# Event places, step orders, the last quarters and the first stacking of keys in a fused attention and FFN kernel

## The reference

```
x = x + xattn(layernorm(x), ctx)          # q, k, v projections, softmax over 1601 keys, output projection and bias
x = x + ffn(layernorm(x))                 # gate and up 256 -> 704, silu(gate) * up, down 704 -> 256
fp4_linear(x, w) = einsum(fp4(x), fp4(w)) # blocks of 16: scale = max|x|/6, values rounded to an FP4 grid
```

## Time and profile before

| | us |
|---|---|
| runs of before | 3369.82, 3375.37, 3386.15 (median 3375.37) |
| the profiled execution | 3376.89 |
| its span | 3375.1 |

### The profile page before, as it was taken

One profiled execution on the slowest core, in us unless ns is written; L12 is line 12 of the kernel. 1 busy time (PEld: TensorE's weight loads), 2 busy tenths in 40 slices (PEclk: granted clock), 3 DMA queues, 4 the chain that ended last, 5 costly groups with the idle time before them and its releaser, 6 DMA issues.

```text
span 3375.1 us, 55778 instructions
## 1 busy us (share of the span) xinstructions
PE 3209.6 (95%) x19606; PEld 1657.6 (49%) x19606; DVE 2698.0 (80%) x6009; ACT 2282.7 (68%) x4692; POOL 1097.4 (33%) x1411
## 2 busy tenths in 40 slices
PE   6899999999999999999999999999999999999996
PEld 4344544545455454544545455454544545454444
DVE  6877788888887878878887888878878888887855
ACT  2666677676766767767676776767767677766761
POOL 0213333243333333324343333333333333332332
PEclk6998999999999999999999999999999999999987
DMA  3332133232222322133232222322133232222200
GB/s 78 71 54 47 36 60 56 35 65 39 52 48 40 66 45 50 36 59 58 35 65 35 51 53 42 64 45 53 35 58 56 35 66 43 46 48 46 41 14 8
DMA packets 120783, 163.29 MB, mean 48 GB/s; under 512 B 47125, under 2 KB 93606, under 8 KB 120506
## 3 DMA queue, kind: packets, MB, share of 16 engines
q1 hardware_dynamic: 120506, 159.73, 27.0%
HBM read 46.22 MB, written 8.39 MB: 16 GB/s over the span
## 4 chain that ended last, share of the span: by engine, by line
PE 72%; DVE 11%; ACT 4%; SPq 4%; DMA 4%; POOL 2%; issue 2%; POOLq 0%; DVEq 0%; ACTq 0%
PE out_ps L1014 17%; PE ring L1001 14%; PE ring L1027 13%; PE ring L964 8%; DVE piece_max L1369 6%; PE ring L975 5%; PE ring L931 3%; PE ring L939 3%; DMA k_stack<-k_parts 2%; ACT probs L1140 2%; SPq L820 2%; PE ring L920 2%; DMA q_stack<-neg_rows 2%; PE ring L955 2%; PE ring L949 1%
## 5 line engine op out<-in xcount | busy, mean ns | idle before, releaser
L1369 DVE TENSOR_REDUCE piece_max<-ring 128x1 f32<-128x402 f32 x4096 | 2072.4, 567 | 454.3 <-PE ring L1027 443.5
L1140 ACT ACTIVATE probs<-ring 128x512 f32<-128x512 f32 (+1 forms) x3328 | 1774.8, 605 | 560.4 <-PE ring L1001 544.5
L1014 PE MATMUL out_ps<-probs,v_ones 128*17 128x512 f32 x6656 | 898.9, 612 | 0.8 <-ACT probs L1140 0.8
L1001 PE MATMUL ring<-q_stack,k_stack 50*128 50x512 f32 (+1 forms) x3328 | 841.3, 469 | 37.2 <-DMA q_stack<-neg_rows 24.7
L1027 PE MATMUL ring<-k_stack,q_stack 48*128 48x402 f32 x4096 | 818.9, 391 | 44.8 <-DMA k_stack<-k_parts 32.9
L1001 PEld LDWEIGHTS ring<-q_stack,k_stack 50*128 50x128 f32 (+1 forms) x3328 | 349.5, 184 | 815.4 <-issue 262.0
L1027 PEld LDWEIGHTS ring<-k_stack,q_stack 48*128 48x128 f32 x4096 | 448.6, 192 | 307.9 <-DVE piece_max L1369 95.7
L964 PE MATMUL ring<-wgu_T,xq_T 128*128 128x512 f32 (+1 forms) x1080 | 252.5, 382 | 1.9 <-POOL xq_T L1474 0.5
L1418 POOL TENSOR_TENSOR h<-h,h_grid 128x704 f32<-128x704 f32 (+1 forms) x68 | 101.6, 1494 | 460.2 <-DVE h_grid L1203 460.2
L964 PEld LDWEIGHTS ring<-wgu_T,xq_T 128*128 128x128 f32 x1080 | 192.7, 188 | 53.2 <-issue 22.8
L1014 PEld LDWEIGHTS out_ps<-probs,v_ones 128*17 128x17 f32 x6656 | 110.7, 95 | 218.6 <-issue 183.5
(11 more groups left out here) (170 smaller groups left out, 2662.6 us busy)
## 6 DMA issues: line engine op xcount, KB each, us to landing
k_stack<-k_parts SPq DMA_DIRECT2D x256, 200.1 KB, 4.7
k_stack<-k_parts SPq DMA_DIRECT2D x256, 100.1 KB, 4.3
ctx_in<-in_ctx SPq DMA_DIRECT2D x47, 384.0 KB, 4.0
q_stack<-q_parts SPq DMA_DIRECT2D x256, 64.0 KB, 2.3
x_in<-in_x SPq DMA_DIRECT2D x16, 512.0 KB, 5.5
q_stack<-q_parts SPq DMA_DIRECT2D x256, 32.0 KB, 2.0
resid<-in_x SPq DMA_DIRECT2D x62, 128.0 KB, 2.7
out<-x SPq DMA_DIRECT2D x62, 128.0 KB, 1.8
```

What stands on the lines that cost most here:

```text
L1001: pe.matmul(ring[0:r, bank(kind, batch, item), :], k_stack[rows, at, m * P:m * P + r], q_stack[rows, at, :], start=True, stop=True).then_i ...
L1014: last = pe.matmul(out_ps[32 * j:32 * j + V1, :], v_ones[0:r, batch % 2, m, PER_GROUP * g + j, :], probs[0:r, prob_slot(batch, step, j), : ...
L1140: act.activation(probs[0:r, prob_slot(batch, step, j), :], ring[0:r, at, :], ACT.Exp, scale=SCORE_SCALE).then_inc(probs_ready, 1)
L1369: dve.tensor_reduce(piece_max[:, g % 2, 2 * u + half, t, c:c + 1], ring[:, at, 0:PW], AX_X, ALU.max).then_inc(pieces_max, 1)
```

## The change

- All the tables of places get new numbers. `STEP_ORDERS` becomes a table by group and step that picks from eighteen orders (`ORDERS`). New in them: a `V` ahead of scores or of `W`, and `w`, which takes the events of the step's first half only.
- In step eight of the third group (counted from nought) all four `k_proj` chunks of the next element stand together (half step 69, before 69, 70, 71, 71); the stacking of its first pair is at 69 instead of 70.
- `EARLY_PIECES` goes from 3 to 2, and these early pieces no longer stand among the start's 64 but behind the first `maxima`.
- In the start the keys of the first two pairs are stacked in two parts, the first 1536 keys as soon as three chunks are projected, and the last 65. SP does pair 0, ACT's queue pair 1. The start's pieces go by quarters of the keys first, so that the last quarter's wait for the last 65 keys comes late. `first_queries` and `first_keys` are new semaphores for this.
- `VECTOR_ROUNDS` becomes `[3]`: the rounding of the tail's quarter 1 moves to POOL. `TAIL_AT` is new.
- Helpers are cached (`lru_cache`), which changes no instruction.

```
-POST_AT = [ [5, 9, 12, ...],  [20, 22, 22, 24, 32, 36, 40, 43, 48, 48, 48, 48, 49, 52, 60, 62, 65], ...
+POST_AT = [ [6, 9, 13, ...],  [20, 22, 22, 22, 30, 39, 40, 43, 48, 49, 49, 49, 50, 53, 60, 61, 64], ...
-PRE_AT = [24, 27, 27, 30, 45, 45, 50, 56, 61, 61, 63, 66, 69, 69, 70, 71, 71, 72, 74, 76, 85, 99]
+PRE_AT = [24, 26, 26, 27, 42, 46, 50, 57, 64, 64, 64, 67, 68, 69, 69, 69, 69, 72, 74, 76, 85, 99]
-STACK0_AT = [18, 70]
+STACK0_AT = [16, 69]
-EARLY_PIECES = 3
+EARLY_PIECES = 2
-STEP_ORDERS = ['P S01 W P S23 P V', 'S01 P W P S23 P V', 'S01 P W S23 P V', ...]
+STEP_ORDERS = [
+    [0, 1, 17, 0, 5, 1, 3, 1, 1, 1, 1, 3, 4],
+    [2, 1, 2, 1, 15, 10, 1, 1, 1, 3, 2, 3, 5],
...
-VECTOR_ROUNDS = [1, 3]
+VECTOR_ROUNDS = [3]
...
+            if kind == "start" and g == PHASES:
+                return n // (2 * QT * PIECES), n // 2 % QT, n // (2 * QT) % PIECES, n % 2
...
+        def stack_keys(eng, of, g, u, a, b, done):
+            at = pair_slot(of, g, u)
+            for half in range(2):
+                rows, to = pair_rows(g, u, half)
+                eng.dma_start(k_stack[to:to + 2 * HEAD_DIM, at, a:b].bitcast(F32), k_parts[rows, :, a:b]).then_inc(done, 16)
+                eng.dma_start(k_stack[to + 2 * HEAD_DIM:to + SROWS, at, a:b].bitcast(F32), k_parts[rows, 0, a:b]).then_inc(done, 16)
+
+        def stack_first_keys(eng, u, part):
+            a, _ = chunk(CHUNKS - 1)
+            if part == 0:
+                eng.wait_ge(split_step, len(VECTOR_SPLITS) + CHUNKS - 1)
+                stack_keys(eng, 0, 0, u, 0, a, first_keys[u])
+            else:
+                eng.wait_ge(first_split, len(VECTOR_SPLITS))
+                stack_keys(eng, 0, 0, u, a, NK, stacked[pair_slot(0, 0, u)])
...
-                if t == c == half == 0:
+                if kind == "start" and g == PHASES:
+                    if u == t == c == half == 0:
+                        pe.wait_ge(first_queries, STACKED)
+                    if t == c == half == 0:
+                        pe.wait_ge(first_keys[u], STACKED // 2)
+                    elif t == half == 0 and c == PIECES - 1:
+                        pe.wait_ge(stacked[at], stacked_until(u))
+                elif t == c == half == 0:
                     pe.wait_ge(stacked[at], stacked_until(pair(batch, g, u)))
```

117 lines of the change are left out of this document (75 added, 42 removed), and 26 rows, old and new, of tables (PIECES_AT, POST_AT, STEP_ORDERS, TAIL_AT).

## The result

| | before | after |
|---|---|---|
| median of the runs, us | 3372.60 (3369.65 to 3386.15) | 3251.89 (3244.27 to 3257.17) |
| profiled execution, us | 3376.89 | 3257.17 |
| its span, us | 3375.1 | 3255.3 |

The ratio is 0.9633, with a 95% interval of 0.9599 to 0.9667.

A forecast was written before the change was run, and what follows sets the result against it. PE, 95% busy, was taken as the bound. From 3376.9 us: maxima waits -18, key waits -25, clock -28, new orders +8, first element -6, last -1, start 0, tail -3, total -73: 3304, range 3278 to 3362.

The forecast's parts named there:

- Place A: Third group's scores waiting for the maxima's rows: more PE work during the transfer removes 18 of 20.0 us.
- Place B: Pieces waiting for the next element's keys to be stacked: more PE work behind the last projection removes 25 of 27.2 us.
- The clock: Middle elements: 35 us lost to PE's lower clock, counted as a price of the two long transfer waits; 28 return.
- The cost of the new orders: Third group: a long projection block, bunched pieces and steps with few or no pieces (bare steps) lose 8 us.
- The step of twelve pieces: Third group: one step would hold twelve pieces, where eight was the most before, taking DVE 6.8 us.
- The start and the first element: Start: about 0 us, first pieces at 36, first scores about 79; first element: 6 us gained from waits and clock.
- some 5 us at about 0.6 each; ... so this is covered: Start: ACT's eight transfer issues delay bias copy and value-weight casts some 5 us, hidden while two pieces wait.
- The transfers' sharing: Start: two queues share the same 16 DMA engines; first pieces taken 1 us later, at 36.
- The tail: After the last element: PE's 10.0 us in two waits for POOL's rounding of `h` shrink, 3 us gained.
- The clock did not stay: Rival, chance 0.17: the transfer waits go but the clock still falls as often; 3330 to 3358 us.
- nothing moved back to `piece_max`: Rival, chance 0.12: DVE's bunches delay the maxima and other waits replace the transfers'; 3360 to 3390 us.
- The rival of a slower kernel: Rival, chance 0.09: the third group's long projection block breaks the feeding of ACT and DVE; 3400 us.

The follow-up runs named there:

- place A undone: Changed kernel with the third group's maxima transpose back behind the 384-column `gate_up`, context transpose and `out_proj` back behind the first score: 3320.6 us.
- both undone: Changed kernel with the old order around the third group's maxima transpose and the old key projections, stacking and following steps: 3394.4 us, ratio 1.0041.
- B undone: Changed kernel with key projections back at half steps 69, 70, 71, 71, stacking at 70, and old orders and pieces in third-group steps 8 to 12: 3328.6 us.

## Why the prediction was right and wrong

**Place A and B: right.** 18 and 25 us were to go, and no wait of either kind is left in the list, so 20.0 and 27.2 went. Place B of after:

```profile
1193.80 1.56 PE L982 MATMUL ring<-ctx_T,wk_sb 128*128 128x512 f32 x9
...
1208.26 0.52 PE L1085 MATMUL ring<-k_stack,q_stack 48*128 48x402 f32 x4
```

```profile
1202.60 0.99 SPq L758 DMA_DIRECT2D k_stack<-k_parts  x1
```

The projections end at 1195.36, and PE has 12.9 us of work up to the piece (12.5 forecast). With the 4.1 us from the last issue to the piece in the earlier trace rows, the chain would end at 1206.7, 11.4 us behind the projections (11.75 forecast); the trace has the last transfer landing at 1207.0. The slack is 1.3 to 1.5 us, and no wait for the keys is listed in any element. The runs with a place undone confirm that these covers are what removes the waits.

**The clock: the size nearly right, the mechanism only half.** 28 us were forecast. The same reckoning (the periods less the clean one) gives 2830.6 - 14 x 199.3 = 40 before and 2722.5 - 14 x 193.9 = 8 after, so 32; by the clock's records it is 39. "A price of the two long waits" holds for place B, where filling the wait with full-row work brought it back. At place A undone it doesn't: with the wait filled, 44 to 50 of 53 us stayed lost, where the changed kernel loses 10. These experiments start from the changed kernel; what the wait at place A cost in clock in the kernel before, where the pieces hardly waited for DVE (2.9 us in 14), was not tested. Each place has its own price, as the run with both undone shows; the forecast had them as one sum of 28.

**The cost of the new orders: the step that failed.** 8 us were to be lost in the bare steps, and nothing was: after's list of waits has no score or piece in it. (The step of twelve pieces that the forecast feared isn't in the tables either; the fullest are two of ten.) This and two more gains sit in the clean period. It fell by 5.3 us, 75 in fourteen elements, where the sum had 43 - 8 = 35. Idle accounts for 4.05 x 14 = 57 of it: the 47 us of the two entries and some 10 of the shorter waits. Those stood in the same list: the five entries below the two came to 19.7 us in fourteen elements before, the two that are left come to 7.8, and the forecast gave them nothing. 1.28 x 14 = 18 us are busy time that became shorter with the same matmuls and the clock at 1.00 in both windows. I have no cause for it. It isn't the same in kernels that differ in one place either: beside idle and clock, elements 1 to 14 hold 2699 us before, 2688 after, 2692 with A undone and 2674 with B undone.

**The start and the first element: wrong in sign.** The failed step is "some 5 us at about 0.6 each; ... so this is covered". ACT's issues took 11.6 us beside SP's, where SP alone had needed 8.2 for the eight of before. The value projection's place "behind two pieces anyway" covered them only up to the first pieces: PE did these at 36.51 and then waited 2.8 us for the weights. And before, a value projection had filled a part of the wait for the keys; now it could not. First pieces were forecast at 36 and came at 36.51; first scores at 79, and came at 84.27. The transfers' sharing, for which the Trainium skill's rule ("DMA: Bandwidth & Descriptors", "Issuing engines are not separate DMA queues") was weighed, is real: 36.51 with two queues and 32.58 with one. My 1 us for it was against the kernel before, where the pieces came at 34.83, and that came true; against the one queue with the early first part it is 3.9, and I never worked that version out. The first element's 6 us didn't come in this trace: from first scores to its end 204.1 us before, 206.2 after. The other kernels with its order took 202.5 to 209, so its gain, if there is one, is smaller than what that stretch varies by.

**The tail: sized too small, 3 for 17 us.** Its waits of PE, 3189 us to the end; before, the waits named `v_ones` were 10.0 us, those named `x_in` 8.5, and `ctx_T` 6.1:

```profile
PE ring L1010 <- POOL x_in L1488: 5.5, 2, 3.4
PE ring L1026 <- ACT probs L1193: 4.3, 1, 4.3
PE ring L1015 <- DVE ctx_T L1315: 3.8, 2, 2.9
PE ring L1023 <- DVE v_ones L1260: 1.4, 1, 1.4
...
PE ring L1023 <- POOL v_ones L1488: 0.3, 1, 0.3
```

```profile
3292.70:3375.10 82.40, 50.77 (x180) 38.90 (x180) 47.99 (x108) 10.97 (x29) 21.68 (x27) 0.79 0.03 8
```

```profile
3189.60:3255.30 65.70, 44.38 (x180) 34.45 (x180) 44.67 (x105) 10.96 (x29) 25.02 (x29) 0.87 0.03 9
```

I looked at one pair of waits of 31.6 us of idle, and took a half of one. Idle fell by 10.3 us in all, and PE's busy time by 6.4 for the same 180 matmuls, with the clock at 0.87 for 0.79. So in the tail, too, the clock rose where waits went, which the forecast counted for the middle alone; that the waits are its cause there was not tested. The fear that POOL pays for the rounding that it took over didn't come true; it is busy 25 of 66 us.

**Rivals.** The clock did not stay, and nothing moved back to `piece_max` in the changed kernel. The rival of a slower kernel was wrong in its mechanism, the block of projections; it is what carries place B. The sum, by its own steps: -73, less 40 for the clean period, 4 for the clock, 14 for the tail and 1 for the last element, plus 13 for the start and the first element, is -119, and 119.8 lie between the two spans.

The range was too narrow below. Even with every term at its best end the sum is 3270, still 18 us above the median. It had no term for the short waits and the rest of the tail, 24 us together, nor for the 18 us of busy time, for which I still have no cause.

## What to carry to other kernels

Take one clean period of the loop, busy and idle, and forecast with all of its idle time, not with the longest waits alone. In a chain over several engines, look at what stands between its links on each helper: with two instructions of POOL between the low parts, a wait of 1.9 us was one of 3.5. Before the queue of a computing engine gets transfers, ask what stands behind them on that engine, and cost each issue by rows in which as much is being transferred.
